# Attention between two slot-mixing layers: maxima taken and turned by query halves, with 26 pairs of lead instead of 48

## What is computed

```
def _L0_attn_ref(x, W_qkv, b_qkv, W_out, b_out):
    B, N, E = x.shape                       # 16, 1024, 256
    H = HEADS                               # 16
    d = E // H                              # 16
    qkv = x @ W_qkv + b_qkv
    q, k, v = jnp.split(qkv, 3, axis=2)
    ...
    energy = jnp.einsum('bqhe,bkhe->bqhk', q, k)
    attn = jax.nn.softmax(energy, axis=-1) / sqrt(E)
    out = jnp.einsum('bihv,bvhd->bihd', attn, v)
    out = out.reshape(B, N, E)
    return out @ W_out + b_out

x = x + 0.5 * _L0_ffn_ref(_layernorm(x, axis=-1), ...)
x = x + _L0_attn_ref(_layernorm(x, axis=-1), L0_attn_W_qkv, ...)
x = x + 0.5 * _L0_ffn_ref(_layernorm(x, axis=-1), ...)
```

## Time and profile before

| | us |
|---|---|
| median of 3 runs | 3625.06 (3622.46 to 3627.05) |
| the profiled execution | 3626.83 |
| its span, first to last instruction | 3625.0 |
| mean granted clock of TensorE in it | 0.969 of full speed |
| busy PE, DVE, ACT, POOL | 3390.5, 3063.3, 2691.5, 1017.9 |
| attention's first exponential to its last | 496.6 to 3218.9 |
| one batch of 64 quads in mid-attention | 170.4 |

### The profile page before, as it was taken

How to read it: one execution, slowest core, us unless ns; L and a number is a source line. 1 busy time by engine, 2 the same in 40 slices (tenths; PEclk the granted TensorE clock), 3 DMA queues, 4 the chain that set the end, 5 groups by cost and what they waited for, 6 DMA issues and landing times. The chain is left out here.

```text
span 3625.0 us, 59853 instructions
## 1 busy us (share of the span) xinstructions
PE 3390.5 (94%) x22282; PEld 1189.5 (33%) x22282; DVE 3063.3 (85%) x4480; ACT 2691.5 (74%) x5252; POOL 1017.9 (28%) x803
## 2 busy tenths in 40 slices
PE   6999379999999999999999999999999999958987
PEld 4645112232323222232323232323232232215653
DVE  6965489999999999999999999999999999807955
ACT  4740048888888888888888888888888888846730
POOL 2310322332323242323232332323242322213310
PEclk8999679999999999999999999999999999989999
DMA  3324502322222222221322222222222221122217
GB/s 103 92 96 193 175 10 69 63 54 54 55 55 54 57 61 56 55 64 45 72 48 72 60 57 57 54 54 55 54 63 55 57 43 54 40 61 69 93 72 301
DMA packets 189651, 263.28 MB, mean 73 GB/s; under 512 B 101217, under 2 KB 141985, under 8 KB 175025
## 3 DMA queue, kind: packets, MB, share of 16 engines
q1 hardware_dynamic: 182272, 224.84, 23.3%
q10 hardware_dynamic: 7088, 34.61, 2.3%
HBM read 121.91 MB, written 51.38 MB: 48 GB/s over the span
## 5 line engine op out<-in xcount | busy, mean ns | idle before, releaser
L1370 DVE TENSOR_REDUCE attn_part_max<-attn_ps 128x2 f32<-128x1024 f32 x2048 | 2445.2, 1221 | 226.6 <-PE attn_ps L1497 183.7
L1611 ACT ACTIVATE attn_probs<-attn_ps 128x512 f32<-128x512 f32 x4096 | 2164.4, 599 | 369.1 <-PE attn_ps L1509 369.1
L1509 PE MATMUL attn_ps<-attn_q_rows,attn_k_rows 50*128 50x512 f16 x4096 | 1263.3, 384 | 37.3 <-ACT attn_probs L1611 19.2
L1497 PE MATMUL attn_ps<-attn_k_rows,attn_q_rows 48*128 48x512 f16 x4096 | 1128.9, 388 | 30.0 <-DVE attn_part_max L1370 26.2
L1523 PE MATMUL attn_ps<-attn_probs,attn_v_ones 128*32 128x512 f32 x8192 | 1093.0, 606 | 0.7 <-ACT attn_probs L1611 0.7
L1509 PEld LDWEIGHTS attn_ps<-attn_q_rows,attn_k_rows 50*128 50x128 f16 x4096 | 307.5, 94 | 1327.0 <-ACT attn_probs L1611 1226.3
L1497 PEld LDWEIGHTS attn_ps<-attn_k_rows,attn_q_rows 48*128 48x128 f16 x4096 | 223.3, 94 | 194.0 <-DVE attn_part_max L1370 178.7
L1523 PEld LDWEIGHTS attn_ps<-attn_probs,attn_v_ones 128*32 128x32 f32 x8192 | 161.3, 108 | 237.9 <-issue 136.9
L1448 PE MATMUL attn_ps<-attn_xn_parts,attn_w_qk 128*128 128x256 f16 x1536 | 215.7, 279 | 10.7 <-DMA attn_xn_parts<-attn_x_parts 10.7
L1301 POOL TENSOR_TENSOR attn_x_res<-attn_x_res,attn_y_sb 128x256 f32<-128x256 f32 x128 | 93.7, 734 | 392.6 <-ACT attn_y_sb L1582 392.6
L1256 POOL CAST attn_max_parts<-attn_max_whole 32x128 f16<-32x128 f32 x64 | 18.0, 281 | 622.1 <-ACT attn_max_whole L1563 600.8
(11 more groups left out here) (167 smaller groups left out, 2532.3 us busy)
## 6 DMA issues: line engine op xcount, KB each, us to landing
attn_q_rows<-attn_parts SPq DMA_DIRECT2D x384, 64.0 KB, 2.2
attn_k_rows<-attn_parts SPq DMA_DIRECT2D x384, 64.0 KB, 2.2
ffn_x_ring<-in_L_attn_x SPq DMA_DIRECT2D x16, 1024.0 KB, 5.7
attn_x_ln<-after_first_ffn SPq DMA_DIRECT2D x16, 1024.0 KB, 5.6
attn_o_packed<-attn_o_sb SPq DMA_DIRECT2D x256, 64.0 KB, 2.3
attn_inv_wide<-inverse_denominators SPq DMA_DIRECT2D x32, 512.0 KB
attn_x_res<-after_first_ffn SPq DMA_DIRECT2D x16, 1024.0 KB, 5.1
after_attention<-attn_x_res SPq DMA_DIRECT2D x16, 1024.0 KB, 8.7
```

The lines of the kernel that those rows point to most:

```text
L1370: dve.tensor_reduce(part_max[:, G % 2, :, j, t, half], pair, AX.X, ALU.max).then_inc(dve_emptied, 1)
L1497: last = pe.matmul(ps[:, bank + e, :], q_rows[rows_e, G % NG, j, t * P:(t + 1) * P], k_rows[rows_e, G % NG, j, half * HALF:(half + 1) * HA ...
L1509: pe.matmul(ps[:, bank, :], k_rows[rows_e, G % NG, h // 2, kt * P:(kt + 1) * P], q_rows[rows_e, G % NG, h // 2, half * HALF:(half + 1) * H ...
L1611: act.activation(probs[:, quad % NQ, h, :], bank_of(s, b0), ACT.Exp, scale=1.0 / (SCALE * SCALE)).then_inc(act_emptied, 1)
```

## The change

- A **window** W takes the place of the group for the maxima: half a group's queries, 16 pairs, 8 quads, so 8 windows a batch. The pairs are reordered so that one query half is complete first (`order_of_max`). The small reduction, the turn, `split_max` and `max_rows` happen once per window, with 16 maxima rows instead of 32.
- `AHEAD` is 26 pairs instead of 48. The turns ride at quads 5, 13, ..., 61 (`RIDES`), on whatever piece is there, or alone.
- `q_rows` is laid out by query halves, so that a q row takes two DMAs of 32 KB where it took one of 64 KB: 18 DMAs a group instead of 12.
- The pieces move in `jobs`, and with them `invert` from quad 10 to 12 (37 stays), `quotient` from 13 to 15 (41 stays), and in batch 0 POOL's normalisation from 9 to 14.
- SP's order is written out anew per batch. The store of the residual rows now stands before the spread of the batch's first two groups.
- The opening has the first eight "qk" pieces first and mixes the "v" pieces and the other four with max pairs.

```
-    AHEAD = SG + 16
+    SW, NW, NM = SG // 2, 2 * NG, NE * NJ * TT // 2
+    AHEAD = SW + 10
...
+    RIDES = (5, 13, 21, 29, 37, 45, 53, 61)
+    QK_QUADS = ((5, 6, 12, 13), (28, 29, 30, 31), (44, 45, 46, 47), (60, 61, 62, 63))
...
-        out = [((22, 23, 24, 25, 26, 32, 33, 34)[t], "project", TT * (b - 1) + t) for t in range(TT)]
+        out = [(19 + t, "project", TT * (b - 1) + t) for t in range(TT)]
...
-            out += [((9, 28, 42, 58)[g] + i, "qk", 4 * (NG * b + g + PREP) + i) for i in range(4)]
...
+        out += [((36, 37, 38, 39, 52, 53, 54, 55)[t], "v", TT * (b + 1) + t) for t in range(TT)]
...
+        return w // (TT // 2 * CHUNKS) % NJ, w // SW * (TT // 2) + w // CHUNKS % (TT // 2), w % CHUNKS
...
-        q_rows = sb("q_rows", [P, NG, NJ, T], F16)
+        q_rows = sb("q_rows", [P, NG, CHUNKS, NJ, HALF], F16)
...
+            def max_rows(W):
+
+                sp.wait_ge(max_low_ready, W + 1)
+                G, half = divmod(W, CHUNKS)
                 for e in range(NE):
                     for n in range(2):
...
+                        sp.dma_start(q_rows[row:row + 1, G % NG, half, :, :],
+                                     max_parts[NM // 2 * e:NM // 2 * (e + 1), n, :]).then_inc(max_loaded[W % NW], 16)
...
+                lay_out_if(b, G + PREP - 1)
+                if b > 0:
+                    pack(b, b, G - 1)
+                max_rows(W + 1)
+                if b > 0:
+                    spread(b, b, KT * b - 1)
+                max_rows(W + 2)
+                lay_out_if(b, G + PREP)
...
+                lay_out_if(b, G + PREP + 1)
+                pack(b, b, G + 1)
+                if b > 0:
+                    sp.wait_ge(y_added, TT * b)
+                    sp.dma_start(rows(x_out, b, b, -1), x_res[:, :, :]).then_inc(stored, 16)
+                spread(b, b, KT * b)
+                max_rows(W + 5)
...
-                    if m == 10 and b0 > 0:
+                    if m == 12 and b0 > 0:
                         invert(b, b0, KT * b0 - 1)
...
-                if w == 0 and h == 0:
-                    wait(pe, max_loaded[G % NG], b, lambda i: 64 * ((G + NG * (i - b0)) // NG + 1))
+                if kt == 0 and h == 0:
+                    W = quad // TT
+                    pe.wait_ge(max_loaded[W % NW], 64 * (W // NW + 1))
```

More of the change, by code:

```diff
@@ L984, in rider @@
-    def rider(kind, n):
-        G, part = divmod(n, 4)
-        return G - PREP + 1 if kind == "qk" and part == 0 and G >= PREP else None
-    opening = ([("fold", 0)] + [("qk", i) for i in range(4)] + [("v", i) for i in range(TT)]
-               + [("qk", i) for i in range(4, 8)] + [("max", v) for v in range(16)] + [("qk", i) for i in range(8, 12)]
-               + [("max", v) for v in range(16, SG + 3)] + [("turn_max", 0)] + [("max", v) for v in range(SG + 3, AHEAD)])
-    closing = [("project", TT * (B - 1) + t) for t in range(TT)]
@@ L994, in build_attention @@
-    RATE = {"score": 4 * QB, "max": SB, "project": TT, "turn_max": NG, "qk": 4 * NG, "v": TT, "fold": 0}
-    act_slot, dve_slot, count = {}, {}, [0, 0]
+            out += [(QK_QUADS[g][i], "qk", 4 * (NG * b + g + PREP) + i) for i in range(4)]
+        out += [((36, 37, 38, 39, 52, 53, 54, 55)[t], "v", TT * (b + 1) + t) for t in range(TT)]
+        out = [j for j in out if 0 <= j[2] < RATE[j[1]] * B]
+        free = [m for m in RIDES if m not in [j[0] for j in out]]
+        out += [(m, "turn_max", NW * b + 1 + RIDES.index(m)) for m in free if NW * b + 1 + RIDES.index(m) < NW * B]
@@ new lines, in jobs, with order_of_max @@
+        return sorted(out)
+    def order_of_max(w):
+        return w // (TT // 2 * CHUNKS) % NJ, w // SW * (TT // 2) + w // CHUNKS % (TT // 2), w % CHUNKS
+    opening = [("fold", 0)] + [("qk", i) for i in range(8)] + [("max", v) for v in range(3)]
+    for i in range(TT):
+        opening += [("v", i), ("max", 3 + i)]
+    for i in range(4):
+        opening += [("qk", 8 + i), ("max", 3 + TT + i)]
+    opening += [("max", SW - 1), ("turn_max", 0)] + [("max", v) for v in range(SW, AHEAD)]
+    closing = [("project", TT * (B - 1) + t) for t in range(TT)]
@@ L997, in enter @@
+    RATE = {"score": 4 * QB, "max": SB, "project": TT, "turn_max": NW, "qk": 4 * NG, "v": TT, "fold": 0}
+    act_slot, dve_slot, count = {}, {}, [0, 0]
+    rides = {}
+    for b in range(B):
+        for m, kind, n in jobs(b):
+            if m in RIDES and kind != "turn_max" and NW * b + 1 + RIDES.index(m) < NW * B:
+                rides[kind, n] = NW * b + 1 + RIDES.index(m)
+    def rider(kind, n):
+        return rides.get((kind, n))
     def enter(kind, n):
@@ L1083, in build_attention @@
         rows_loaded = [sem(f"rows_loaded{g}") for g in range(NG)]
-        max_loaded = [sem(f"max_loaded{g}") for g in range(NG)]
+        max_loaded = [sem(f"max_loaded{w}") for w in range(NW)]
         neg_max_ready, max_high_ready, max_low_ready = sem("neg_max_ready"), sem("max_high_ready"), sem("max_low_ready")
@@ L1199, in turn_x, with lay_out_if @@
                                            x_parts[:, part].rearrange("p t d -> p (t d)")).then_inc(xn_turned, 16)
+            def lay_out_if(b, G):
+                if PREP <= G < NG * B:
+                    lay_out(b, b, G)
             turn_x(0)
             load_x(1)
[L1203 removed]
+            for G in range(2):
                 lay_out(0, 0, G)
[L1205 to L1229 removed]
@@ L1230, in _ @@
-            over_batches(sp, body, (act_slot["score", 4 * QB * 3] - act_slot["score", 4 * QB * 2], 2, NG, 2 * NG, 16))
+            max_rows(0)
+            lay_out(0, 0, 2)
+            for b in range(B):
+                G, W = NG * b, NW * b
+                lay_out_if(b, G + PREP - 1)
[6 more added lines that the diff above has]
+                lay_out_if(b, G + PREP)
+                if b + 1 < B:
+                    turn_x(b + 1)
+                if b + 2 < B:
+                    load_x(b + 2)
+                pack(b, b, G)
+                max_rows(W + 3)
+                max_rows(W + 4)
+                lay_out_if(b, G + PREP + 1)
[5 more added lines that the diff above has]
+                max_rows(W + 5)
+                if b > 0:
+                    sp.wait_ge(stored, 16 * b)
+                sp.dma_start(x_res[:, :, :], rows(x_in, b, b)).then_inc(res_loaded, 16)
+                max_rows(W + 6)
+                lay_out_if(b, G + PREP + 2)
+                pack(b, b, G + 2)
+                max_rows(W + 7)
+                if b + 1 < B:
+                    max_rows(W + 8)
@@ L1310, in _ @@
             split_x(0)
-            for G in range(PREP):
+            for G in range(PREP - 1):
                 split(0, 0, G)
@@ L1440, in dve_pair, with turn_rider @@
                 return 2 * (s(b0) % 2)
+            def turn_rider(kind, n, bank, last):
+                W = rider(kind, n)
+                if W is None:
+                    return last
+                pe.wait_ge(neg_max_ready, W + 1)
+                return pe.transpose(ps[0:NM, bank, 2 * P:3 * P], neg_max[:, W % 2, :], c.ident[:, :])
             def project_qk(b, b0, n):
```

155 lines of the change are left out of this document (63 added, 92 removed).

## The result

| | before | after |
|---|---|---|
| median of the runs, us | 3626.06 (3622.46 to 3627.12) | 3859.26 (3856.14 to 3862.22) |
| ratio, 95% interval | | 1.0645 (1.0626 to 1.0663) |
| span of the profiled execution, us | 3625.0 | 3857.9 |
| first exponential at, us | 496.57 | 471.09 |
| first to last exponential, us | 2722.3 | 2982.9 |

The change makes the kernel 6.4% slower. The opening gives back 25.5 us, the 16 batches take 260.6 more, and what follows the attention is the same within 2.2.

A forecast was written before the change was run, and what follows sets the result against it. The ring of three score banks between PE and ScalarE was taken to set the pace. 3626.8 - 21.5 (opening) + 11 (batch 0) + 200 (steady batches) + 14 (batch 15) = 3830, forecast 3829 us; 8-in-10 range 3672 to 3890.

The forecast's parts named there:

- opening: Before the first exponential: 26 pairs instead of 48, against a later first pair and slow first pieces; -21.5 us (-17 to -24).
- steady batches: Batches between the first and last: riders plus waits at quads 16 and 40 with clock, +14.3 us each, 14 times, +200.
- W+1: Max rows of a batch's second window, for quad 8: landing at 22.9 us against 23.3, so in time.
- W+2: Max rows for quad 16, behind the spread after the reciprocal moves to quad 12: late by 4.3 us, clock 0.5.
- W+5: Max rows for quad 40, behind residual store and spread: late by 8.0 us (5.5 to 13.3), clock 1.1.
- riders: Eight turns of maxima a batch on ScalarE instead of four: +0.4 us a batch.
- batch 0: First batch: old stall's 6.2 us goes; late 8.3 + 1.1 at quad 24, 6.0 + 1.1 at 40, turns 0.8: +11.
- batch 15: Last batch: 4.8 us at quad 16, 6.8 + 1.1 at quad 40, 1.1 for turns riding on nothing: +14.
- W+3: Max rows for quad 24: landing at 31.4 us against 30.1 + 4.3, so in time, with no term in the sum.
- Rival 1: Smaller max rows slip past inv_wide and land 1.8 us after issue: 3676 us, chance 0.17.
- Rival 2: More waits are late than found, as SP has little spare time; 5 us a batch more: 3905 us, chance 0.13.
- Rivals 3 and 4: Rival 3: all lands in time, only the lead counts, 3611 us, chance 0.04. Rival 4: gains and stalls cancel, 3625, 0.03.

The follow-up runs named there:

- experiment 5: Experiment 4's kernel with W+3's max rows moved ahead of the 1 MB load and pack(G) on SP's queue: 3620.7 us, ratio 0.9983.
- experiment 7: Experiment 5's kernel with W+1's rows ahead of pack(G-1) and x(1)'s statistics, normalising and splitting done in the opening: 3611.7 us, ratio 0.9954.
- experiment 3: The changed kernel with a batch's first reciprocal at quad 9 instead of 12, nothing else: 3863.5 us, ratio 1.0657.
- experiment 4: The changed kernel with first reciprocal at quad 9, W+5's rows before spread and residual store, bias added at quad 48: 3695.8 us, ratio 1.0193.
- experiment 2: The changed kernel with inverse rows stored twice, so inv_wide's broadcast has extent 16 instead of 8: 3832.1 us, ratio 1.0571.

## Why the prediction was right, and where not

The forecast was 3829 us and the time is 3859, inside the range, and the mechanism is the one forecast. By its own steps:

| step | forecast | measured |
|---|---|---|
| opening | -21.5 | -25.5 |
| steady batches, 14 | +200 (14.3 each) | +234 (16.7 each) |
| of these W+1 | 0 | 0.9 |
| W+2, with clock | 4.8 | 4.9 |
| W+5, with clock | 9.1 | 10.6 |
| riders and the rest | 0.4 | 0.7 |
| batch 0 | +11 | +12.3 |
| batch 15 | +14 | +14.3 |
| the rest of the span | 0 | -2.2 |

(The rows of single windows are means over batches 2 to 13, which stand at 17.1 in all.)

*The opening.* The layout's 18 DMAs were to delay the first pair by 3.8 us: it came 1.4 later here, and the kernels with this same opening had it anywhere from 437.3 to 442.6. My + 2.7 for PE's first pieces is about 3.1 by its own figures (1.9 less 1.13, four times). From the first pair to the first exponential the change is steady, 58.94 to 32.03 or -26.9, where I had -25.3.

*W+2* was right in its sum by luck, as two errors cancel: the rows were there by S(13) + 11.2 (1829.61 less 1818.38), not 12.06, since they landed 8.6 us after inv_wide's issue and not 9.5, and the lower clock took 1.2 us, not 0.5.

*W+5* is the mis-sized term. On the mean of batches 2 to 13 the store left at S(38) + 1.9, not + 0.8, and inv_wide at + 6.8, not + 4.8: from the store's issue to inv_wide's it was 4.8 us, where I had 4.0. Then the rows came 8.0 us after inv_wide's issue, not 9.0. That is + 14.7 for + 13.8. Batch 7, with S(38) at 1890.63, is near it in the sum and not in the parts: + 1.4, + 6.8, + 14.8. Excess at quad 39 was 9.15 for 8.0, and the clock cost 1.5 for 1.1.

*W+1* I had called in time by 0.4 us, on a chain of 23 us. It was late by 0.9, in experiment 5 too, until its rows went ahead of the pack in experiment 7.

*W+3 was the real mistake*, and it cost the forecast nothing. I wrote "31.4 against 30.1 + 4.3": in time only because quad 16 had already lost 4.3. That means W+3 is late by itself, by 1.3 on my own figures, and I gave it no term. Then the true statement is that a wait at quad 16 or one at quad 24 costs about 5 us a batch, and not both. For the changed kernel the sum is the same. For any mend of it (experiments 3 and 4) it is wrong by 75 us, and it was. With the wait of quad 16 gone, the rows were issued at S(13) + 29.1 and PE released at + 32.9 (1782.07 and 1785.88 less 1753.00), with S(24) at + 29.6: late by 3.3. In the changed kernel the same rows landed at + 33.4 on the mean, with S(24) pushed to + 34.5 by quad 16's wait.

*Rival 1* (the smaller max rows slip past inv_wide) fell. The rows land with inv_wide's eight parts, and cutting inv_wide in sixteen (experiment 2) moves both. *Rival 2* (more is late) was right as to W+1, but with 0.9 us a batch for its 5. *Rivals 3 and 4* needed waits under 1.3 us a batch. The change can get there, but only with SP's order and the reciprocal's place mended (experiments 5 and 7).

## What to carry to other kernels

A shorter lead is bought with the slack of every small transfer behind it. List the deadlines one by one, each with what its queue carries ahead of it, before moving work. A margin that holds only because an earlier deadline is missed is a wait in waiting: write it down as one, since any mend of the first will bring it out, and a mend that gains nothing has not shown that its cause was wrong. Rows that a later stage waits for belong ahead of loads and packs with time to spare, and a store, a wait for it and a broadcast in one queue were 13 us to the rows behind them here (1892.06 to 1905.4).
